# Two attention loops run as one program, with four-piece projections, half tiles in the last experts and the key casts on ScalarE

## The reference

```python
    x = x + _L0_xattn_ref(_layernorm(x, axis=-1), ctx_1024, ctx_1024, L0_xattn_Wq, ...)
    x = x + _L0_ffn_ref(_layernorm(x, axis=-1), L0_ffn_Ws, ...)
    x = x + _L1_xattn_ref(_layernorm(x, axis=-1), ctx_1024, ctx_1024, mask_SxS2_bk0, L1_xattn_Wq, ...)
    x = x + _L1_ffn_ref(_layernorm(x, axis=-1), L1_ffn_Wq, ...)
    return x
```

```python
    def _attention(x, Wq, bq, Wk, bk, Wv, bv, Wo, bo):
        q = (x @ Wq + bq).reshape(b, s, H, dh)
        k = (x @ Wk + bk).reshape(b, s, H, dh)
        v = (x @ Wv + bv).reshape(b, s, H, dh)
        scores = jnp.einsum('bqhd,bkhd->bhqk', q, k) / math.sqrt(dh)
        attn = jax.nn.softmax(scores, axis=-1)
        out = jnp.einsum('bhqk,bkhd->bqhd', attn, v).reshape(b, s, d)
        return out @ Wo + bo
    def _moe(x, gate_w, gate_b, W1, b1, W2, b2):
        xt = x.reshape(b * s, d)
        probs = jax.nn.softmax(xt @ gate_w + gate_b, axis=-1)
        top_v, top_i = jax.lax.top_k(probs, K)
        combine = jnp.sum(jax.nn.one_hot(top_i, E, dtype=xt.dtype) * top_v[..., None], axis=1)
        for e in range(E):
            h = jax.nn.gelu(xt @ W1[e] + b1[e], approximate=False) @ W2[e] + b2[e]
            out = out + combine[:, e:e + 1] * h
    x = x + _layernorm(_attention(x, Wq, bq, Wk, bk, Wv, bv, Wo, bo), ln1_g, ln1_b)
    x = x + _layernorm(_moe(x, gate_w, gate_b, W1, b1, W2, b2), ln2_g, ln2_b)
```

## Time and profile before

| | us |
|---|---|
| median of 3 launches | 2672.95 (2672.91 to 2680.4) |
| the profiled execution | 2670.24 |
| its span | 2668.5 |
| PE busy in it | 2281.8 (86%) |
| DVE busy | 1322.2 (50%) |
| ScalarE (ACT) busy | 1007.1 (38%) |
| POOL busy | 765.5 (29%) |

### The profile page before, as it was taken

How to read it: one execution, slowest core, us unless ns; L and a number is a source line. 1 busy time by engine, 2 the same in 40 slices (tenths; PEclk the granted TensorE clock), 3 DMA queues, 4 the chain that set the end, 5 groups by cost and what they waited for, 6 DMA issues and landing times. The chain is left out here.

```text
span 2668.5 us, 38158 instructions
## 1 busy us (share of the span) xinstructions
PE 2281.8 (86%) x10840; PEld 1270.4 (48%) x10840; DVE 1322.2 (50%) x3459; ACT 1007.1 (38%) x1807; POOL 765.5 (29%) x772
## 2 busy tenths in 40 slices
PE   6877399967999999996799999999737999999990
PEld 2554266642333333332233434333336888888880
DVE  5547534215776676772577767677472111111115
ACT  2222022202655555553165555555502323222222
POOL 4117323332111111100423323323112333333335
PEclk9988699986999999998699999999958999999995
DMA  4326434425222222300434324234006666666654
GB/s 156 115 101 225 142 108 111 102 49 141 58 49 44 49 54 49 57 13 23 48 49 57 48 36 56 40 51 57 9 8 180 183 189 178 190 174 190 179 155 132
DMA packets 199817, 257.10 MB, mean 96 GB/s; under 512 B 21424, under 2 KB 177584, under 8 KB 197616
## 3 DMA queue, kind: packets, MB, share of 16 engines
q1 hardware_dynamic: 177968, 224.89, 33.2%
q0 software_dynamic: 21696, 30.42, 6.6%
HBM read 163.52 MB, written 53.20 MB: 81 GB/s over the span
## 5 line engine op out<-in xcount | busy, mean ns | idle before, releaser
L1911 DVE CUSTOM_DVE_ANT_0 atL1x_junk<-atL1x_pm,bias 128x512 bf16<-128x512 f32 x512 | 343.9, 687 | 179.1 <-PE atL1x_pm L1580 164.7
L1907 DVE TENSOR_REDUCE atL_tops<-atL_pm 128x1 f32<-128x512 f32 x512 | 339.4, 683 | 177.9 <-PE atL_pm L1580 170.2
L1178 PE MATMUL exL_po<-exL_w,exL_hid 128*128 128x256 f32 x1760 | 393.2, 382 | 16.9 <-DVE exL_ys L1243 8.9
L1162 PE MATMUL exL_ph<-exL_xgT,exL_w 128*128 128x256 f32 (+1 forms) x1504 | 397.4, 420 | 6.0 <-ACT exL_hid L1194 3.6
L1739 ACT ACTIVATE atL1x_prob<-atL1x_ps 128x512 f32<-128x512 f32 x512 | 303.4, 598 | 260.5 <-PE atL1x_ps L1597 248.1
L1739 ACT ACTIVATE atL_prob<-atL_ps 128x512 f32<-128x512 f32 x512 | 294.9, 599 | 258.9 <-PE atL_ps L1594 256.4
L1178 PEld LDWEIGHTS exL_po<-exL_w,exL_hid 128*128 128x128 f32 x1760 | 330.0, 190 | 71.4 <-issue 16.7
L1194 ACT ACTIVATE exL_hid<-exL_ph,exL_b 128x256 f32<-128x256 f32 (+1 forms) x376 | 189.9, 510 | 432.0 <-PE exL_ph L1162 431.8
L1162 PEld LDWEIGHTS exL_ph<-exL_xgT,exL_w 128*128 128x128 f32 x1504 | 275.5, 191 | 112.2 <-issue 59.2
L1128 POOL DMA_INDIRECT sum<-exL_ys,exL_put x110 | 180.0, 1637 | 423.9 <-DVE exL_ys L1243 244.6
L1580 PE MATMUL atL1x_pm<-atL1x_kstack,atL1x_qstack 96*128 96x512 bf16 x512 | 201.9, 396 | 17.8 <-DMA atL1x_qstack<-atL1x_q 9.7
(11 more groups left out here) (331 smaller groups left out, 2691.4 us busy)
## 6 DMA issues: line engine op xcount, KB each, us to landing
exL_w<-in_L_W SPq DMA_DIRECT2D x94, 1024.0 KB, 5.2
kstack<-pick_k SPq DMA_DIRECT2D x48, 256.0 KB, 3.0
atL1x_kstack<-kstack SPq DMA_DIRECT2D x16, 768.0 KB, 7.6
atL1x_qstack<-atL1x_q SPq DMA_DIRECT2D x96, 128.0 KB, 4.6
atL_kstack<-atL_k SPq DMA_DIRECT2D x96, 128.0 KB, 4.6
atL_qstack<-atL_q SPq DMA_DIRECT2D x96, 128.0 KB, 6.9
exL_b<-in_L_b SPq DMA_DIRECT2D x47, 128.0 KB, 5.4
values<-pick_vals SPq DMA_DIRECT2D x8, 574.0 KB, 4.6
```

Source lines behind the costliest of these rows:

```text
L1162: mm = pe.matmul(ph[f % 2][:], w1[slot][:, m, f * P:(f + 1) * P], xgT[:, m, :], start=m == 0, stop=m == DC - 1)
L1178: mm = pe.matmul(po[c % 2][:], hid[:, f, c * P:(c + 1) * P], w2[slot][:, f, :], start=f == 0, stop=f == FC - 1)
L1907: ins = dve.tensor_reduce(tops[g % 2][:, t, j:j + 1], pm[i % TOPS][:], AX.X, ALU.max)
L1911: ins = dve.tensor_tensor_reduce(junk[:, i % TOPS, :], pm[i % TOPS][:], G["bias"][0][:, t, :], 1.0, -BIG / 2, ALU.add, ALU.max, tops[g % 2 ...
```

## The change

Five things are changed.

1. `attention` is one program for both. Its batches are cross 0, a loop over cross 1 to 6, cross 7 with the jobs for self 0, self 0 with those behind cross 7, a loop over self 1 to 6, and self 7. Self's weights and the bias fold stand in the part before cross batch 0, behind the loads of x, keys and values. `u2` is gone: `add_y` writes into `yn`, which SP stores, and DVE waits before the job y0 for that store and for POOL's last addition. `vals` needs no memset, since the values' frame is loaded in cross attention.
2. The jobs k1, q1, v0, v1, y0 and y1 have four pieces of one matmul of 256 columns where they had two pieces of two matmuls, and begin later: k1 at step 22 (21), q1 28 (24), v0 35 (27), v1 41 (30), y1 16 (14), out0 21 (20).
3. In `expert_choice` ScalarE makes the two casts, and POOL only the subtractions.
4. The experts of layer 1 have 35 tiles of 256 rows and 4 of 128 behind them, in place of 39 of 256. Up to four experts whose last tile would hold at most 128 rows have it among the half tiles. The loop covers 32 tiles; seven stand behind it.
5. `top_experts` has the operations that this needs, and the lists are 76 columns wide where they were 82.

```diff
-TILES = {"L0": E * CAP // TILES_OF["L0"], "L1": (N * TOPK + E * (TILE - 1)) // TILE}
-COLS = (TILES["L1"] + 2) * TILE // P
+HALVES = E // 2
+UNITS = (N * TOPK + E * (P - 1)) // P
+WHOLE = max((UNITS - halves) // 2 + max(0, halves - HALVES) for halves in range(E + 1))
+TILES = {"L0": E * CAP // TILES_OF["L0"], "L1": WHOLE + HALVES}
+COLS = WHOLE * TILE // P + HALVES + 2
...
-                        act.copy(kf[b % 2][:, o, :], pk[o][:]).then_inc(k_saved, 1)
+                            act.wait_ge(k_out[b % 2], past(b // 2 * KOUT))
+                        act.copy(kf[b % 2][:, o, :], pk[o][:])
+                        act.copy(kparts[b % 2][0][:, o, :], pk[o][:]).then_inc(k_saved, 1)
+                    for o in range(DC):
+                        act.wait_ge(k_rest, past(b * DC + o + 1))
+                        act.copy(kparts[b % 2][1][:, o, :], kf[b % 2][:, o, :]).then_inc(k_mid, 1)
...
-                        chain(pool.tensor_copy(hi, x_))
-                        chain(pool.tensor_tensor(x_, x_, hi, ALU.subtract))
-                        chain(pool.tensor_copy(mid, x_))
+                        pool.tensor_tensor(x_, x_, hi, ALU.subtract).then_inc(k_rest, 1)
+                    for o in range(DC):
+                        x_, (hi, mid, lo) = kf[b % 2][:, o, :], (p[:, o, :] for p in kparts[b % 2])
+                        pool.wait_ge(k_mid, past(b * DC + o + 1))
                         pool.tensor_tensor(lo, x_, mid, ALU.subtract).then_inc(k_cut, 1)
...
+        whole = tiles if early else WHOLE
+        looped = tiles // 2 if early else (WHOLE - 2) // 2
+
+        def chunks(t):
+            return 1 if isinstance(t, int) and t >= whole else TC
+
+        def begins(t):
+
+            return whole * TC + t - whole if isinstance(t, int) and t > whole else t * TC
...
-                            mm = pe.matmul(ph[f % 2][:], w1[slot][:, m, f * P:(f + 1) * P], xgT[:, m, :],
+                            mm = pe.matmul(ph[f % 2][:, 0:n * P], w1[slot][:, m, f * P:(f + 1) * P], xgT[:, m, 0:n * P],
...
-                    for c in range(TC):
-                        pe.wait_ge(ys_ready, past(t * TC + max(c - 1, 0)))
+                    for c in range(n):
+                        pe.wait_ge(ys_ready, past(begin + max(c - 1, 0)))
...
-                        act.activation(hid[:, f, :], ph[f % 2][:], gelu, bias=b1[slot][:, f:f + 1]).then_inc(hid_ready, 1)
+                        act.activation(hid[:, f, 0:n * P], ph[f % 2][:, 0:n * P], gelu, bias=b1[slot][:, f:f + 1]).then_inc(hid_ready, 1)
...
-PIECES = {"k": 2, "q": 2, "v": 2, "y": 2, "l": 2}
+PIECES = {"k0+": 2, "q0+": 2, "k1+": 4, "q1+": 4, "v0+": 4, "v1+": 4, "y0-": 4, "y1-": 4, "logits-": 2}
...
-def job_table(self_, first, last):
+def job_table(prev_self, next_self):
 
     jobs = [(7, "d", "neg1"), (23, "d", "neg2"), (39, "d", "neg3"),
-            (20, "d", "out0"), (36, "d", "out1"), (52, "d", "out2")]
-    if not last:
+            (21, "d", "out0"), (36, "d", "out1"), (52, "d", "out2")]
+    if next_self is not None:
         jobs += [(11, "a", "turn0+"), (13, "a", "turn1+"), (55, "d", "neg0+")]
-    if not last and self_:
-        jobs += [(15, "a", "k0+"), (18, "a", "q0+"), (21, "a", "k1+"), (24, "a", "q1+"), (27, "a", "v0+"), (30, "a", "v1+")]
-    elif not last:
+    if next_self:
+        jobs += [(15, "a", "k0+"), (18, "a", "q0+"), (22, "a", "k1+"), (28, "a", "q1+"), (35, "a", "v0+"), (41, "a", "v1+")]
+    elif next_self is False:
         jobs += [(15, "a", "q0+"), (18, "a", "q1+")]
-    if not first:
-        jobs += [(4, "d", "out3-"), (7, "a", "att0-"), (9, "a", "att1-"), (11, "d", "y0-"), (14, "d", "y1-")]
-        if self_:
-            jobs += [(47, "a", "u0-"), (50, "a", "u1-"), (57, "d", "logits-")]
+    if prev_self is not None:
+        jobs += [(4, "d", "out3-"), (7, "a", "att0-"), (9, "a", "att1-"), (11, "d", "y0-"), (16, "d", "y1-")]
+    if prev_self:
+        jobs += [(47, "a", "u0-"), (50, "a", "u1-"), (57, "d", "logits-")]
...
-            before()
-            batch(0, 0)
+            before(Where(-1, False, None, False, start=True))
+            batch(Where(0, False, None, False), 0)
             with eng.Fori(0, (B - 2) // 2) as pair:
-                batch(pair * 2 + 1, 1)
-                batch(pair * 2 + 2, 0)
-            batch(B - 1, 1)
-            behind()
...
+                batch(Where(pair * 2 + 1, False, False, False), 1)
+                batch(Where(pair * 2 + 2, False, False, False), 0)
+            batch(Where(B - 1, False, False, True), 1)
+            batch(Where(0, True, False, True), 0)
+            with eng.Fori(0, (B - 2) // 2) as pair:
+                batch(Where(pair * 2 + 1, True, True, True), 1)
+                batch(Where(pair * 2 + 2, True, True, True), 0)
+            last = Where(B - 1, True, True, None)
+            batch(last, 1)
...
+                    load_x(slice(CB, NC), "x_rest")
+                    load_weights()
+                    fill(w, 0, 0)
+                    fill(w, 0, 1)
...
+                def project(w_, x_, o, cols, m):
+                    return pe.matmul(pj["a"][:, cols], w_[:, m, o * P:(o + 1) * P], x_[:, m, cols],
+                                     start=m == 0, stop=m == DC - 1)
...
-                    pool.tensor_tensor(u2[:], yn[:], ukept[par][:], ALU.add).then_inc(s["u_ready"], 1)
-                    pool.wait_ge(s["u_ready"], past(b + 1))
+                    pool.tensor_tensor(yn[:], yn[:], ukept[par][:], ALU.add).then_inc(s["u_ready"], 1)
+                    pool.wait_ge(s["u_ready"], past(of.rows + 1))
...
+                            if i == 0 and not (isinstance(of.rows, int) and of.rows == 0):
+
+                                dve.wait_ge(s["rows_stored"], past(of.rows * 16))
+                                dve.wait_ge(s["u_added"], past(of.rows))
...
+                chain(dve.scalar_tensor_tensor(out=full[:], in0=to(sizes, [P, E, N // TILE], 2), scalar=-float(P),
+                                               in1=to(steps[:], [P, E, N // TILE], 1), op0=ALU.add, op1=ALU.is_gt))
+                chain(dve.tensor_reduce(large[:], full[:], AX.X, ALU.add))
+                chain(dve.tensor_tensor(half[:], size[:], large[:], ALU.subtract))
...
+                chain(dve.tensor_tensor(late[:], inside, to(whole[:], [P, E, NC], 2), ALU.is_ge))
+                chain(dve.tensor_tensor(late[:], late[:], to(jump[:], [P, E, NC], 2), ALU.mult))
+                chain(dve.tensor_tensor(at[:], at[:], late[:], ALU.add))
...
-        attention(nc, G, a, "L1x", False)
-        attention(nc, G, a, "L1", True)
+        attention(nc, G, a)
```

891 lines of the change are left out of this document (445 added, 446 removed).

## The result

The changed kernel takes 2603.82 us (median of 4, 2600.94 to 2607.64) where the kernel before takes 2672.93: a ratio of 0.9739, 95% interval 0.9714 to 0.9764. It is faster, by 69 us, but 32 us less fast than forecast, and outside the range of 2548 to 2600. The profiled execution shows where.

What follows compares the result with a forecast made beforehand. PE was taken to bound attention and layer 1's experts, a loop through four engines the key stage. Gains 67 + 7 + 8 + 24.6, less 5 and 3, make 98.6: 2670.24 us becomes 2572, range 2548 to 2600.

Steps and rivals of the forecast that it cites:

- The seam: From cross batch 7 to self batch 1: merging the programs takes 152.1 us in place of 219.0, a gain of 67.
- C: Rival between cross and self: self batch 0's cuts and stacks come late, seam gains 55, spreading 0; 2591 us, chance 0.08.
- D: Rival between cross and self: the merged program still drains, saving some 15 of the 67 us; 2624 us, chance 0.03.
- E: Rival in the attention batches: without the pause, the clock falls to 1.2 GHz; at two batches 2717 us, chance 0.02.
- The spreading: Attention projections in more pieces at later steps fill PE's idle time: 7 us gained, bounds 20 gained to 12 lost.
- the prediction's own sign of being wrong: In attention: the prediction is wrong if steady batches move by over 3 us either way.
- The casts: In the stage that makes the keys: casts on ScalarE shorten the loop, 8 us gained, bounds 3 to 14.
- The half tiles: In layer 1's experts: four half tiles take 8.8 us each instead of 14.95, 24.6 gained, bounds 12 to 27.
- the two readings of the Trainium skill's rule on weight loads: In a half tile's first part: weight loads alone need 3.4 us, or 7 if loads and matmuls did not overlap.
- The prologue: Ahead of cross batch 0: twelve more weight loads transfer ahead of the first stacks, 5 us lost, bounds 0 to 9.
- The routing: In layer 1's routing: more small DVE operations, partly offset by narrower lists, 3 us lost, bounds 1 to 5.

Runs made afterwards that it cites:

- old_table: The changed kernel with all projections back in two pieces and at the old steps: 2591.28 us, ratio 0.9704.
- before_spread: The kernel before with only the four pieces and later steps added, still two programs, whole tiles and old casts: 2690.05 us, ratio 1.006.
- kf_weights: The changed kernel with POOL's `keep` ahead of the second cut, self's weight loads behind both first stacks, and the bias fold behind the second maxima: 2574.91 us, ratio 0.9634.
- keep_first: The changed kernel with POOL's `keep` (its addition into ukept) moved ahead of the second cut: 2577.07 us, ratio 0.9646.
- keep_late: The changed kernel with `keep` ahead of the second cut and the next sequence's keys loaded later, about step 8 of a cross batch: 2574.77 us, ratio 0.9644.
- keep_four: The changed kernel with `keep` at its old place but as four additions of 256 columns instead of one of 1024: 2584.19 us, ratio 0.9662.
- before_half: The kernel before with only the half tiles added (experts, top_experts, lists of 76 columns): 2662.83 us, ratio 0.9954.
- mixed_late: The changed kernel with `keep` ahead of the second cut, cross jobs in two pieces at old steps, next keys loaded about step 8: 2589.28 us, ratio 0.9691.
- half_late: The kernel before with only the half tiles, and the next sequence's keys loaded later in a cross batch: 2653.45 us, ratio 0.9931.

## Why the prediction was wrong, point by point

- **The seam**: right, 151.9 us for 152.1 forecast, at a granted clock of 1.00. Cross batch 7 took 81.5 (80.5 forecast), self batch 0 70.3 (71.6). Rivals C, D and E did not come; E's mechanism did, in another place.
- **The spreading**: the step that failed. Taken as 7 us gained, with a bound of 12 lost; the cross and self batches that it was priced for came 22.3 longer (3.8 and 18.5), and the prediction's own sign of being wrong, steady batches off by over 3 us, came with 5.1. Taken back by itself the spreading costs less: old_table is 12.5 us faster than the changed kernel, since it gains 21.6 in the six self batches and pays 10.7 in the cross batches, at the turns; added to the kernel before (before_spread) it costs 15. Either way it is a loss where a gain was forecast. Two things in it. The bound priced the pieces on PE only. The prediction read PE and DVE for room in the third quarter, and said that "the rest lies where POOL and the router are late, which no piece touches"; but lengthening a quarter shifts POOL's operations against DVE's. The earlier trace rows gave POOL's share and not where it lies. The trace of before had the sign of it: three of the four operations that cut the maxima in the fourth quarter, 0.16 to 0.22 us long in other kernels here, took 0.54, 0.79 and 0.54 there, each while one of POOL's cuts ran. The first two:

```profile
1447.73 0.61 POOL L1770 CAST atL_k<-atL_kf 128x512 bf16<-128x512 f32 x1
1447.83 0.54 DVE L1924 TENSOR_SCALAR atL_neg<-atL_tops 128x16 bf16<-128x16 f32 x1
1448.49 1.16 POOL L1771 TENSOR_TENSOR atL_k<-atL_kf,atL_k 128x512 bf16<-128x512 f32 x1
1448.89 0.79 DVE L1928 SCALAR_TENSOR_TENSOR atL_rest<-atL_tops,atL_neg 128x16 f32<-128x16 f32 x1
```

  And the clock was thought of as one rival over whole batches, not as 10 us that each of six batches can lose when PE is thin for a few microseconds. Without the collision the term is small but there: kf_weights' self batch 9, at full clock and away from a turn, is 74.53 us where the kernel before has 75.58, the 1 us forecast; old_table's, without the spreading, is 75.30, so 0.3 of it comes from elsewhere. In cross it is a loss of 0.6 a batch where 0.2 of gain was forecast: the second quarter there has 0.1 us of idle PE before, and gets 1.85 us longer, while the first gets 1.25 shorter.

```profile
1324.50:1399.03 74.53, 69.81 (x386) 30.79 (x385) 55.87 (x125) 44.56 (x82) 25.96 (x24) 1.00 0.38 51
```

- **The casts**: right in mechanism, 6.7 us earlier at the stage's end for 8 forecast. PE's wait for the source came down from 4.93 us to 2.4 at most.
- **The half tiles**: right. The four tiles follow each other after 8.64 us (8.8 forecast). The second part takes 3.72 us where the prediction had 3.45, and the first 4.62, above the 4.4 that ScalarE was reckoned to give and the 3.4 or 3.7 by weight loads. Of the two readings of the Trainium skill's rule on weight loads ("TensorE: Matmul & The Clock Gate", section "LDWEIGHTS"), the one without overlap (7 us) is refuted by this row, and the other was never what bounds:

```profile
2504.96 4.62 PE L1183 MATMUL exL_ph<-exL_xgT,exL_w 128*128 128x128 f32 x32
2510.04 3.72 PE L1199 MATMUL exL_po<-exL_w,exL_hid 128*128 128x256 f32 x16 [0.24 <-ACT exL_hid L1216]
2513.60 4.62 PE L1183 MATMUL exL_ph<-exL_xgT,exL_w 128*128 128x128 f32 x32
```

- **The prologue**: forecast 5 us lost, measured 6.7 (the attention begins 8.0 us earlier, its first exponential 1.3). The mechanism was another: not the weights' transfer ahead of the stacks, but SP, which issued no second weight load before 607.07 and then had eleven more to issue, so that the stacks, cut by 607.15, were issued 6.7 us later. That this is the whole loss is not shown: kf_weights, without it, got 2.2 us of it back.
- **The routing**: forecast 3, measured 2.5.
- **The range**: 2548 to 2600 left 2603.8 out since the spreading's worst end was 12 us lost. The ends were added as the root of their squares, 26 us; with the 22 lost that were measured in its place the same sum gives 34, and 2606 holds the result. The end was too near because the bound knew of PE alone.

The version that I would keep is keep_first (2577), keep_late (2575) or kf_weights (2575), 27 to 29 us faster than the change and 3.5 to 3.7% faster than the kernel before; which of the three, these runs don't tell.

## What to carry to other kernels

Before moving work by steps, look at every engine whose operations shift with it, and for each long POOL operation at which short DVE operation it will stand beside; split the long one, or put it where DVE reads PSUM (in keep_first DVE's maxima, read from PSUM beside `keep`, kept their 0.69 us). A small wait on a nearly full PE costs its length, and behind some of them the clock fell for 7 to 14 us, at half speed: look at the granted clock by quarter, not by stage. And when one part of a change is timed alone, compare the stages that it doesn't touch as well: here a loop that no line had changed took 12 us more, and hid 8 of a true gain of 20.

## What the runs showed of the hardware

- A DVE cast of 128x16 that takes 0.16 us took 2.26 to 2.29 just behind the start of a POOL addition of 2.36 (changed kernel), 0.64 to 0.66 behind that of one of 0.73 (keep_four), and 0.23 where a POOL subtraction ended 0.03 us before it did (keep_first). Each time it ended some 0.03 us behind POOL's operation. DVE's maxima of 128x512, read from PSUM, took 0.69 beside the same addition.
- With PE near full, a late start of about 2 us on DVE was followed by 10 to 14 us at 1.2 GHz in five of six batches of the changed kernel and 7 in the sixth; the granted clock fell within 1.7 us of the router's matmuls of 8 columns. Without the late start it fell there in one of six (keep_first) and in four of six (keep_late), for 10 us each time; in keep_first it fell for 7 us too at each of the two turns of the self loop, where PE stood 3.7 and 3.5 us.
- Turning back the cross loop cost 5 to 7 us or 11 to 13, by kernel, and both in one pair of kernels with the same attention code (before and before_half). Moving 1.5 MB of DMA away from the turn took 3.7 to 5.5 us off the dearer ones (mixed_late, half_late), and 3.0 and 0.2 off the two cheap ones of keep_late.
